# GELU written to SBUF instead of in place in PSUM, with reordered turns and end, in a three-stage macaron kernel

## The reference, cut to what matters

```python
def _ternary_linear(x, w):                 # ffn weights: w_q is -1, 0 or 1
    alpha = jnp.mean(jnp.abs(w))
    w_t = jnp.sign(w) * (jnp.abs(w) > 0.5 * alpha)
    rms = jnp.sqrt(jnp.sum(x * x, axis=-1, keepdims=True)) / jnp.sqrt(d)
    return jnp.einsum('bsd,fd->bsf', x / (rms + EPS), w_t)
ffn(x)  = _ternary_linear(gelu(_ternary_linear(x, w_up)), w_down)
attn(x): log_f, log_i = log_sigmoid(x Wf), log_sigmoid(x Wi); log_h~ = log_g(x Wh)
         h_t = f_t * h_(t-1) + i_t * g(h~_t), h_0 = 0.5     # written there as a scan of logaddexp
x = x + 0.5 * ffn(layernorm(x))            # first ffn,  w_up 512x128, w_down 128x512
x = x + attn(layernorm(x))                 # a gated recurrence along 256 steps
x = x + 0.5 * ffn(layernorm(x))            # second ffn, the same weights
```

## Time and profile before

| what | value |
|---|---|
| median of 3 runs | 263.3 µs (263.24 to 263.63) |
| the profiled execution | 263.04 µs |
| its span in the trace | 261.3 µs |
| busy share of the span: PE, DVE, ACT, POOL | 91%, 90%, 85%, 83% |

### The profile page before, as it was taken

How to read it: one execution, slowest core, us unless ns; L and a number is a source line. 1 busy time by engine, 2 the same in 40 slices (tenths; PEclk the granted TensorE clock), 3 DMA queues, 4 the chain that set the end, 5 groups by cost and what they waited for, 6 DMA issues and landing times.

```text
span 261.3 us, 9753 instructions
## 1 busy us (share of the span) xinstructions
PE 236.6 (91%) x3759; PEld 167.1 (64%) x3759; DVE 234.1 (90%) x754; ACT 221.4 (85%) x534; POOL 216.4 (83%) x400
## 2 busy tenths in 40 slices
PE   0759999999998899899999998679999999999992
PEld 0626777777777667655555544357777776777782
DVE  3798799999999998999999999986999999988784
ACT  2377999989998899879999997997899999999861
POOL 5676998989998898599999999998889989997133
PEclk9988999999999999999999999999999999999999
DMA  6990000000000000000000000000111211112114
GB/s 188 300 265 3 4 4 3 3 3 4 3 3 4 3 4 4 3 0 1 3 1 0 0 1 3 3 3 3 43 43 57 67 46 43 43 43 82 46 43 123
DMA packets 18062, 9.73 MB, mean 37 GB/s; under 512 B 608, under 2 KB 17888, under 8 KB 18016
## 3 DMA queue, kind: packets, MB, share of 16 engines
q1 hardware_dynamic: 17744, 8.98, 12.5%
q10 hardware_dynamic: 272, 0.13, 0.2%
HBM read 4.92 MB, written 4.19 MB: 35 GB/s over the span
## 4 chain that ended last, share of the span: by engine, by line
PE 53%; DVE 21%; ACT 7%; POOL 7%; issue 6%; DVEq 0%; ACTq 0%; POOLq 0%
PE Y L502 17%; PE U L458 9%; PE G L489 9%; PE U L459 8%; DVE hidden L701 5%; PE T L439 4%; ACT h_hi L330 4%; DVE st L719 3%; DVE h_lo L654 3%; PE U L518 2%; DVE cand L691 2%; DVE mv L619 2%; PE G L478 2%; POOL xn L236 2%; POOL root L212 2%
## 5 line engine op out<-in xcount | busy, mean ns | idle before, releaser
L654 DVE SCALAR_TENSOR_TENSOR h_lo<-h_hi,U 128x1024 f16<-128x1024 f16 x63 | 75.6, 1215 | 10.0 <-ACT h_hi L330 9.6
L324 ACT ACTIVATE U<-U 128x1024 f32<-128x1024 f32 x63 | 64.7, 1026 | 15.3 <-PE U L459 14.4
L236 POOL TENSOR_SCALAR xn<-X,neg_mean,rstd 128x128 f32<-128x128 f32 x156 | 67.8, 447 | 6.9 <-DVE rstd L624 4.2
L330 ACT ACTIVATE h_hi<-U 128x1024 f16<-128x1024 f32 x63 | 64.7, 1027 | 1.0
L502 PE MATMUL Y<-down_w,h_hi 128*128 128x128 f16 x496 | 59.4, 220 | 0.0
L502 PE MATMUL Y<-down_w_half,h_lo 128*128 128x128 f16 x496 | 59.0, 219 | 0.0
L458 PE MATMUL U<-xt_hi,up_w 128*128 128x512 f16 x128 | 49.2, 384 | 9.4 <-DVE h_lo L654 7.5
L212 POOL TENSOR_TENSOR root<-mv,half 128x8 f32<-128x8 f32 x31 | 51.0, 1644 | 2.3
L459 PE MATMUL U<-xt_lo,up_w 128*128 128x512 f16 x128 | 49.2, 384 | 0.0
L502 PEld LDWEIGHTS Y<-down_w_half,h_lo 128*128 128x128 f16 x496 | 48.5, 98 | 0.4
L502 PEld LDWEIGHTS Y<-down_w,h_hi 128*128 128x128 f16 x496 | 47.7, 98 | 1.6
(11 more groups left out here) (101 smaller groups left out, 415.2 us busy)
## 6 DMA issues: line engine op xcount, KB each, us to landing
X<-in_L_attn_x SPq DMA_DIRECT2D x16, 256.0 KB, 5.3
out_x<-X SPq DMA_DIRECT2D x15, 256.0 KB, 2.8
up_raw<-in_L_ffn_w_up SPq DMA_DIRECT2D x1, 256.0 KB, 4.5
down_raw<-in_L_ffn_w_down SPq DMA_DIRECT2D x1, 256.0 KB, 4.7
out_x<-X SPq DMA_DIRECT2D x1, 128.0 KB, 1.9
out_x<-X ACTq DMA_DIRECT2D x1, 128.0 KB, 2.9
gate_raw<-in_L_attn_Wh SPq DMA_DIRECT2D x1, 64.0 KB, 3.7
gate_raw<-in_L_attn_Wi SPq DMA_DIRECT2D x1, 64.0 KB, 3.6
```

What stands on the lines that cost most here:

```text
L236: m = eng.tensor_scalar(xn[:, n % 2, t, :], X[:, c, :], neg_mean[l][:, c:c + 1], rstd[l][:, c:c + 1], ALU.add, ALU.mult)
L324: eng.activation(U[part][:], U[part][:], ACT.Gelu, scale=1.0 / XN_SPLIT).then_inc(gelu_done, 1)
L330: eng.mul(h_hi[:, F % 2, 2 * part:2 * part + 2, :], U[part][:], H_SPLIT).then_inc(h_hi_done, 1)
L654: vec.scalar_tensor_tensor(out=h_lo[:, F % 2, 2 * part:2 * part + 2, :], in0=h_hi[:, F % 2, 2 * part:2 * part + 2, :], scalar=-1.0 / H_SPL ...
```

## The change

1. GELU writes a new float32 SBUF tensor H (two buffers by round) instead of U; `h_high` and `h_low` read H. `up` then waits for GELU (gelu_done) instead of h_lo_done, and GELU of round F waits for `h_low` of round F-2.
2. From group 6 on, the first network's norm statistics go through POOL two groups at a time (`links`): one root instruction on 128x16 values instead of two on 128x8, and likewise for the small steps; DVE's `scales` follow.
3. First turn: the gates of group 0 and one of group 1 wait for GELU instead of h_lo and stand ahead of `gram(15)`; the other two gates of group 1 follow `gram(15)` and `down(15)`, with other PSUM banks (`z`). The diagonals of round 14 are taken by DVE instead of ACT (`diagonal_by_max`).
4. Second turn: DVE adds the last recurrence result before the statistics of the group ahead.
5. End: `gram(31)` is cut into four pieces placed among the rows of `down(30)`; `down(31)` signals after two rows and after four; group 14 is added half by POOL and half by DVE, and stored in two DMAs of 128 KB instead of one of 256 KB.

```diff
+        H = sb("H", [P, 2, chunks, GT])
+        def z(g):
+            return [Z[1][0], Z[0][0], Z[1][1]] if g == 1 else Z[g % 2]
+        def links(l):
+            singles = 6 if l == 0 else groups
+            return [(l, g, 1) for g in range(singles)] + [(l, g, 2) for g in range(singles, groups, 2)]
         def diagonal_by_max(F):
-            return F >= 2 * groups - 4
+            return F >= 2 * groups - 4 or F == groups - 2
...
             def gelu(F, part):
                 act.wait_ge(up_ready, 2 * F + part + 1)
-                eng.activation(U[part][:], U[part][:], ACT.Gelu, scale=1.0 / XN_SPLIT).then_inc(gelu_done, 1)
+                if F >= 2:
+                    act.wait_ge(h_lo_done, 2 * F - 3 + part)
+                eng.activation(H[:, F % 2, 2 * part:2 * part + 2, :], U[part][:], ACT.Gelu, scale=1.0 / XN_SPLIT).then_inc(gelu_done, 1)
...
-                eng.mul(h_hi[:, F % 2, 2 * part:2 * part + 2, :], U[part][:], H_SPLIT).then_inc(h_hi_done, 1)
+                eng.mul(h_hi[:, F % 2, 2 * part:2 * part + 2, :], H[:, F % 2, 2 * part:2 * part + 2, :], H_SPLIT).then_inc(h_hi_done, 1)
...
-                    pe.wait_ge(h_lo_done, 2 * F + part - 1)
+                    pe.wait_ge(gelu_done, 2 * F + part - 1)
...
-                                         scalar=-1.0 / H_SPLIT, in1=U[part][:], op0=ALU.mult, op1=ALU.add).then_inc(h_lo_done, 1)
+                                         scalar=-1.0 / H_SPLIT, in1=H[:, F % 2, 2 * part:2 * part + 2, :], op0=ALU.mult, op1=ALU.add).then_inc(h_lo_done, 1)
...
-            gram(2 * groups - 1)
-            down(2 * groups - 1)
+            down(LAST - 1, [0])
+            last_gram(0)
+            last_gram(1)
+            last_gram(2)
+            down(LAST - 1, [1])
+            last_gram(3)
+            down(LAST - 1, [2, 3])
+            down(LAST)
```

More of the change, by code:

```diff
@@ L70, in build_macaron @@
         var_eps = sb("var_eps", [P, 2, TILES])
-        root = [sb(f"root{l}", [P, 2, TILES, 2]) for l in range(3)]
-        den = [sb(f"den{l}", [P, 2, TILES]) for l in range(3)]
+        root = [sb(f"root{l}", [P, 2, 2 * TILES, 2]) for l in range(3)]
+        den = [sb(f"den{l}", [P, 2, 2 * TILES]) for l in range(3)]
         xn = sb("xn", [P, 2, TILES, d])
@@ L145, in cols, with link_of @@
             return slice(g * TILES, g * TILES + n)
+        def links(l):
+            singles = 6 if l == 0 else groups
+            return [(l, g, 1) for g in range(singles)] + [(l, g, 2) for g in range(singles, groups, 2)]
+        def link_of(l, g):
+            return next(i for i, (_, first, n) in enumerate(links(l)) if first <= g < first + n)
         def by_both(n):
@@ L218, in first_roots @@
                 pool.wait_ge(var_first, 1)
-                eng.tensor_tensor(root[0][:, 0], mv[0][:, cols(0), 1:3], half[:], ALU.pow).then_inc(root_done[0], 1)
+                eng.tensor_tensor(root[0][:, 0, 0:TILES, :], mv[0][:, cols(0), 1:3], half[:, 0:TILES, :], ALU.pow).then_inc(root_done[0], 1)
             def rnn_scales(g):
@@ L242, in rms_step @@
                 pool.wait_ge(ssq_done, F + 1)
-                eng.tensor_tensor(rms[:, par, :], ssq[:, par, :], half[:, :, 0], ALU.pow).then_inc(rms_ready, 1)
+                eng.tensor_tensor(rms[:, par, :], ssq[:, par, :], half[:, 0:TILES, 0], ALU.pow).then_inc(rms_ready, 1)
                 pool.wait_ge(rms_ready, F + 1)
@@ L479, in gram @@
                               start=True, stop=False, tile_position=(0, n * HALF))
[L480 to L490, removed]
@@ L491, in gram, with products @@
-                m.then_inc(gram_done, 1)
+            def products(F, t, c, last):
+                for right in (h_hi, h_lo):
+                    for n in range(2):
+                        e = slice(t * P + n * HALF, t * P + (n + 1) * HALF)
+                        m = pe.matmul(gram_of(F)[n * HALF:(n + 1) * HALF, t, 0:HALF], h_hi[:, F % 2, c, e], right[:, F % 2, c, e],
+                                      start=False, stop=last and right is h_lo, tile_position=(0, n * HALF))
+                return m
@@ L493, in down, with last_gram @@
+            def last_gram(c):
+                pe.wait_ge(h_lo_done, 2 * LAST + max(c, 1))
+                if c == 0:
+                    mask(LAST)
+                for t in range(TILES):
+                    m = products(LAST, t, c, t == TILES - 1 and c == chunks - 1)
+                if c == chunks - 1:
+                    m.then_inc(gram_done, 1)
             def down(F, rows=range(TILES)):
@@ L558, in _ @@
                 turn(groups + r + 1)
-                gates(r)
+                if r != 1:
+                    for n in range(3):
+                        gate(r, n)
                 if r >= 1:
@@ L794, in _ @@
                     finish_ffn(k, q)
-                later_stats(s)
+                if s != 2 * groups:
+                    later_stats(s)
                 if 0 <= r - 1 < groups:
                     add_rnn(r - 1)
+                if s == 2 * groups:
+                    later_stats(s)
+                if not in_ffn:
+                    finish_ffn(k, q)
                 if 29 <= s < 2 * groups:
```

167 lines of the change are left out of this document (101 added, 66 removed).

## The result

The changed kernel takes 303.0 us (median of 4 runs, 301.7 to 303.6) against 263.3 us: 1.150 times as long, 95% interval 1.147 to 1.154. 291 us had been forecast, in a range of 257 to 312. The profiled execution spans 299.7 us against 261.3, 38.4 more.

A forecast was written before the change was run, and what follows sets the result against it. POOL, as full as PE in the second network, was taken to set the pace under holds. 17.4 + 13.1 - 0.3 - 0.8 - 1.2 is +28 on 263.0: 291 us, range 257 to 312.

The forecast's parts named there:

- The first rival: Whole kernel: POOL and DVE read side by side without holds, so it gets faster, 257.5 us; chance 0.29.
- the third: Whole kernel: a hold of some 0.5 a round cancels against the other terms' gains, 263 us; chance 0.06.
- The hold of 1.7 a round: POOL's rounds: instructions falling due during an h_lo start when it ends, costing 1.7 us a round, bounds 0.9 to 2.4.
- Second network, +17.4: Second network: 11 rounds held 1.7 us each, less the 1.3 us an xn is ready before PE turns it.
- A pow under way goes on: POOL's root and rms: one already running when an h_lo starts is not disturbed and doesn't hold DVE.
- the second rival: Whole kernel: each h_lo keeps POOL out for its whole 1.215 us, pows included, xn keep DVE out; 311 us, chance 0.15.
- H on ACT at nothing: ACT: GELU writing H to SBUF and h_hi reading it there cost 0.
- U's release at nothing under holds: PE's up no longer waiting for h_lo is worth nothing with holds, as POOL sets the pace; 3 us without.
- First network, +13.1: First network: ten paired rounds cost 9.3 us, three single ones before them 5.1, less 1.3.
- First turn, -0.3: First turn: gates come about 2 us earlier but DVE lacks time; -0.3 us, between +0.4 and -0.8.
- Second turn, -0.8: Second turn: gram(16) no longer waits 0.78 us for the last addition; -0.8 us, bounds 0 and -2.
- End, -1.2: End: gram(31) earlier, rms hidden, POOL's last addition halved, last stores smaller; -1.2 us, between 0 and -2.

The follow-up runs named there:

- The run with the PSUM comparison: Changed kernel, but h_lo compares h_hi with raw U in PSUM, and up and the first gates wait for h_lo; 264.4 us, ratio 1.005 to the kernel before.
- The two runs with the moved turn: turn(18) put ahead of down(15) and gate(1,2): in the changed kernel without H 260.8 us, in the changed kernel with H 300.5 us.
- the fastest version: Changed kernel without H (GELU in place in PSUM), with turn(18) ahead of down(15) and gate(1,2); 260.8 us, ratio 0.991 to the kernel before.

## Why the prediction was right, and where it was off

*The direction and the mechanism* were right: an instruction of POOL that falls due under an h_lo with two SBUF inputs waits for its end, and PE, ACT and DVE wait behind it. The first rival (no holds; its terms add up to 257.7, not 257.5) and the third fell with the first trace. That the second SBUF input is the cause is shown by the run whose h_lo reads U from PSUM.

*The hold of 1.7 a round* measured 1.61 in the second network and 1.60 in the first without pairs. The walk had den and rms_den held; it is rms_den and xn. It set the phase of h_lo by xn, turn, xt_hi and h_hi. In the trace DVE starts the round at den, with rstd, xt_lo and then both h_lo in one go, so the first falls due as rms ends. The size was right, the place was not.

*Second network, +17.4*: measured +15.1 in the ten rounds and +0.4 behind them. The prediction counted 11 rounds with a root; the trace before has ten (rms at 176.63 to 233.99), and ten holds of 1.7 less the lead of 1.3 would have been 15.7. Ten holds of 1.61 are 16.1; the rounds grew by 1.0 less because one of them had been longer before (6.60), with a wait of 0.90 that is gone.

*A pow under way goes on*: right, root and rms kept 1.65 and 1.01 nearly everywhere. The forecast did not say what happens to a pow that falls due under an h_lo: it is held like any other (2.64 above). Of the second rival, full holds, two parts are true: this one, and that an h_lo grows longer when it begins under an xn tile, 1.38 here and 1.41 at worst in the changed kernel. The mean is 1228 against 1215, so DVE's share in the loss is small. The Trainium skill, SBUF — State Buffer, section SBUF: two separate sides, lets whichever of the two instructions starts first keep the other out for the whole instruction. The rows agree where an h_lo is first (0.74 and 0.87 held) and where an xn tile is (the h_lo of 1.38 began 0.30 before the tile's end and is 0.16 longer). They do not where a root is first, since an h_lo that began 0.35 us into it still took 1.22. Nor do they where the two start almost together: in the changed kernel a tile issued at 16.38 takes 1.52 and the h_lo begun at 16.44 its usual 1.23, so the later one won.

*H on ACT at nothing*: GELU 1022 against 1026, h_hi 28 ns more for each of 63, 1.8 us in all. The run with the PSUM comparison has the same longer h_hi (1058) and takes 264.4 against 263.8 without H, so most of it was covered. *U's release at nothing under holds*: right within the spread of the runs (303.8 without it).

*First network, +13.1*: measured +15.7 to the first inject. The second rms comes 5.0 later (37.51 against 32.54), where three single rounds were sized at 5.1. The ten rounds with pairs behind it, from 37.51 to the end of the tenth xn at 103.71, take 6.62 each, sized at 6.57: 9.8 more than ten of 5.64, where 9.3 was forecast. mv, neg_mean and one root of sixteen values are held there as well; an undisturbed root of sixteen takes 2.91, close to the 2.93 that the prediction had worked out. So what was mis-sized is the lead: 1.3 had been taken off for it, and the way from there to the first inject is 0.9 longer instead.

*First turn, -0.3*: this step failed. The recurrence became 3.9 longer, by the new order alone (55.40 with H alone, 58.99 without H). I had costed what the gates gain by starting early and not what they were moved past: turn(18) came to stand behind `down(15)` and a gate, and ACT's queue, which runs in order, kept sigmoids whose input was ready behind a copy whose input was not. The two runs with the moved turn show this for 2.7 of 3.6 without H and for 1.65 of 3.9 with it; the rest stays open.

*Second turn, -0.8*: this failed too; with H it is +4.0. The sum charged the 11 rounds with an rms for their holds and left out the two rounds of the turn, which have xn, mv and no rms: xn takes 2.71 and 3.76 instead of 1.74 and mv 1.15 instead of 0.20, together 3.9. The run with H alone, in the old order, has the same 4.0. Without H the last inject to the first rms is 11.66 in the fastest version and 11.65 before, and ten rounds from there take 56.50 against 57.36: the 0.8 gained comes in the round behind.

*End, -1.2*: measured -0.7, and -0.8 in the fastest version (20.8 against 21.6 from the last xn). The last addition is 0.73 instead of 1.26.

*The sum.* Predicted +28.2, measured +38.4 between the two profiled executions: 2.6 from the first network, 4.2 from the first turn, 2.9 from second turn and second network taken together (17.4 - 0.8 against 4.0 + 15.1 + 0.4), 0.5 from the end. 303 lies between the forecast and the second rival's 311, but the latter's mechanism (pows under way held) is not what made it so. That the hold came out right in size at another place than the walk had it is luck, and both turns were wrong in sign.

## What to carry to other kernels

When an instruction's operand is moved between memories, ask which engine beside it reads from the same memory, and look at what that engine does in that time: a neighbour without gaps pays the whole overlap, one that is inside a long instruction on few values pays nothing, and cutting the instruction helps only if a gap is left between the pieces. Look for the loss in the durations of the neighbour, since a held instruction shows no wait. And when an order is rewritten, cost each instruction by what it was moved behind, on its own engine and on the in-order queue that takes its result.

## What was not expected of the hardware

- A held POOL instruction has its start where it was issued and a longer duration: rms_den of 0.19 shows 0.93, one xn tile of 0.44 shows 1.81.
- Between four h_lo pieces back to back POOL's step of 0.2 us got through at the first seam, and its tile of 0.44 not at the second or third; what the tile gains at a seam is some 0.08 us (an estimate).
- An xn tile and an h_lo that start within 0.1 us of each other: the tile waits, though it was issued first (16.38 and 16.44 in the changed kernel).
- An h_lo and a root of eight elements a partition overlap freely when the root is first (1.22 and 1.65), and the root pays what is left of the h_lo when it is second (2.64).
- ACT writes GELU to SBUF and to PSUM in the same time (1022 and 1026 ns); reading 1024 float32 elements a partition from SBUF instead of PSUM cost it 28 ns.
